# Four GNN layers on one core: rows without links on 49 dense groups by index, the rest of them in idle link slots

## The reference

```
edge_index = jnp.stack([src, dst])
x = _layernorm(x + _L0_gnn_ref(x, edge_index, ...))
x = _layernorm(x + _L1_gnn_ref(x, src, dst, ...))
x = _layernorm(x + _L2_gnn_ref(x, edge_index, ...))
x = _layernorm(x + _L3_gnn_ref(x, edge_index, ...))
```

## Time and profile before

| | |
|---|---|
| timed runs | 6511.86, 6522.25, 6542.76 us (median 6522.25) |
| span of the profiled execution, first to last instruction | 6136.9 us |
| median less the span | 385.4 us |
| TensorE, VectorE, ScalarE, GpSimd busy | 5167.8, 4560.9, 3817.9, 3041.7 us |
| mean granted TensorE clock | 0.886 |

### The profile page before, as it was taken

The page is one execution under the profiler, slowest core; times in us unless marked ns, Lnnn a source line. Parts: engine busy times, 40 slices in busy tenths (PEclk is TensorE's granted clock), DMA queues, the critical chain, the costliest instruction groups (busy, mean ns, idle before and its releaser), DMA issues. The chain is left out here.

```text
span 6136.9 us, 94789 instructions
## 1 busy us (share of the span) xinstructions
PE 5167.8 (84%) x23690; PEld 3888.2 (63%) x23690; DVE 4560.9 (74%) x13038; ACT 3817.9 (62%) x11901; POOL 3041.7 (50%) x2581
## 2 busy tenths in 40 slices
PE   2788899999999988888888998988899989945654
PEld 1566666666677776767666666667777767733443
DVE  7676655555677787887787888878878777768886
ACT  0587765666899766666655555565555567755555
POOL 1677777422444455555355665543333230057776
PEclk7899999999999999999988888889999989955555
DMA  1577543343566554545344444434544431134442
GB/s 49 183 266 255 193 136 113 125 142 112 195 221 220 184 183 165 190 171 183 137 141 155 157 154 159 161 109 141 166 153 152 137 109 54 39 115 138 139 138 94
DMA packets 362734, 925.74 MB, mean 151 GB/s; under 512 B 66872, under 2 KB 140715, under 8 KB 362198
## 3 DMA queue, kind: packets, MB, share of 16 engines
q1 hardware_dynamic: 271078, 702.73, 33.4%
q0 software_dynamic: 91120, 216.96, 12.1%
HBM read 568.39 MB, written 361.72 MB: 152 GB/s over the span
## 5 line engine op out<-in xcount | busy, mean ns | idle before, releaser
L2207 POOL DMA_INDIRECT got<-hop,end_i x600 | 642.6, 1071 | 725.0 <-PE psum L1014 466.0
L2207 POOL DMA_INDIRECT got<-tab,end_i x600 | 702.8, 1171 | 441.7 <-PE psum L1122 266.7
L1122 PE MATMUL psum<-got,sf 128*128 128x264 f32 (+2 forms) x1200 | 470.4, 482 | 365.0 <-DVE got L1946 288.4
L1014 PE MATMUL psum<-got,sf 128*128 128x256 f32 x1600 | 507.1, 399 | 104.8 <-ACT got L1278 96.8
L1122 PEld LDWEIGHTS psum<-got,sf 128*128 128x128 f32 x1200 | 238.8, 240 | 470.6 <-DVE got L1946 350.4
L1014 PEld LDWEIGHTS psum<-got,sf 128*128 128x128 f32 x1600 | 289.5, 195 | 269.4 <-issue 99.8
L2298 POOL DMA_INDIRECT out<-res,out_i x200 | 211.4, 1057 | 463.9 <-DMA out<-hd 358.0
L963 PE MATMUL psum<-h_t,w 128*128 128x512 f32 x784 | 380.3, 616 | 68.5 <-DVE h_t L1705 68.5
L1162 ACT ACTIVATE squares<-res,l_sv 128x256 f32<-128x256 f32 x600 | 297.3, 496 | 223.7 <-DVE l_sv L1851 188.7
L1278 ACT COPY got<-psum 1x256 f32<-1x256 f32 x796 | 280.0, 352 | 239.2 <-PE psum L1014 184.2
L1316 ACT ACTIVATE res<-res,l_mo 128x256 f32<-128x256 f32 x600 | 310.8, 589 | 147.7 <-DVE l_mo L1839 147.5
(11 more groups left out here) (438 smaller groups left out, 14914.2 us busy)
## 6 DMA issues: line engine op xcount, KB each, us to landing
own<-hop SPq DMA_DIRECT2D x150, 512.0 KB
x_t<-res SPq DMA_DIRECT2D x150, 512.0 KB
xo<-x_t SPq DMA_DIRECT2D x150, 512.0 KB, 3.7
hop<-res SPq DMA_DIRECT2D x100, 512.0 KB
x_in<-in_x SPq DMA_DIRECT2D x98, 512.0 KB, 4.6
out<-hd SPq DMA_DIRECT2D x98, 512.0 KB
tab<-tab SPq DMA_DIRECT2D x50, 536.0 KB, 2.7
own<-tab SPq DMA_DIRECT2D x50, 536.0 KB
```

The lines of the kernel that those rows point to most:

```text
L1014: T.matmul(o, sf_of(q)[:, k * P:(k + 1) * P], got_of(q)[:, k * FEAT:(k + 1) * FEAT], start=(p < 3), stop=True).then_inc(at("l_agg"), 1)
L1122: T.matmul(bank(3 + k % 2)[:, 0:g.ext], sf_[:, k * P:(k + 1) * P], got_of(q)[:, k * g.width:k * g.width + g.ext], start=True, stop=True).t ...
L2207: eng.indirect_dma_start(out=dst, out_offset=None, in_=table, in_offset=bass.IndirectOffsetOnAxis(ap=idx, axis=0), bounds_check=rows_ - 1, ...
```

## The change

1. `nd` falls from 98 to 49: `nd = ceil((n - 126 * 200) / 512)`. A list `ulist` of the rows without links is made at run time. Its first 25,088 rows are the dense groups; they are fetched and written by index, by GpSimd: `xin` and `dst` are each four indirect DMAs in place of one SyncE transfer.
2. The other rows without links (about 5,200) are put into link slots that are not the last of their destination. `rank_t` tells which; in pass 0 a compare (`oh`), four matmuls of one column (`oh`) and two additions (`node`) turn ranks into row numbers `node_i` and `out_i`, per link group, ahead of `own`.
3. So that a hosted row sees its loop alone: the 0/1 matrix gets a second half (`s8` and its DRAM copy are twice as wide; `sel` compares twice, `selm` reads the second half), and `hostc` is added to the loop logits (`es`, and one more operation in `sl`).
4. The picking of edges is three streams: `l` (links), `u` (rows without links, new), `o` (old loop table), each of ten `pack` steps on 586 words, with 10 indirect DMAs each. The weights are prepared behind them, in small parts. Dense groups wait for `wz`, for `uct` and for all `emito`.
5. The first `out` no longer waits for dense stores.

```diff
-    nd = -(-n // ROWS)
+    nd = -(-(n - (LINKS - 1) * nt) // ROWS)
-    ready = ("V", "prep", 0)
+    ready = ("V", "wz", 0)
-        if d >= 2:
-            add(("Y", "xin", d), 0.4, [("T", "x0", d - 2), ("T", "x1", d - 2)], landing=4.0)
+        add(("G", "xin", d), 4.8, [ ("T", "x0", d - 2), ("T", "x1", d - 2)], landing=2.5)
-            add(("T", "x", d), 0.6, [("Y", "xin", d), ready], ...)
+            add(("T", "x", d), 0.6, [("G", "xin", d), ("V", "uct", 0), ready] + [("G", "emito", i) for i in range(bits)], ...)
-        add(("Y", "dst", d), 0.35, [("S", "ln", d)] + ..., landing=3.0)
+        add(("G", "dst", d), 4.8, [("S", "ln", d)], landing=2.5)
...
+    stream("l", -1.0, [("Y", "edges", 0), ("G", "prep", 0)], -1.0)
+    stream("u", -0.9, [("V", "edgesl", 0)], -0.9)
+    stream("o", 0.3, [("V", "edgesu", 0)], -0.8)
...
+                put(("Y", "rnk", q), 0.4, s + prior("Yrnk") + ..., landing=4.0)
+                put(("V", "oh", q), 0.65, here("Yrnk") + ...)
+                put(("T", "oh", q), 1.2, here("Voh") + [("V", "uct", 0)], bank="ring", emptied=here("Vnode"))
+                put(("V", "node", q), 0.35, here("Toh"))
-                put(("G", "own", q), 5.2, s + prior("Gown") + gone(b, used), landing=2.5)
+                put(("G", "own", q), 5.2, s + here("Vnode") + prior("Gown") + gone(b, used), landing=2.5)
-                put(("V", "sel", q), 0.68, ...)
+                put(("V", "sel", q), 1.37, ...)
-                over = [("Y", "dst", d) for d in range(max(0, nd - 3), nd)] if i == 0 else [("G", "out", q - 1)]
+                over = [("G", "out", q - 1)] if i else []
...
+        def gpsimd_dense(eng, name, d):
+            if name == "xin":
+                if d >= 2:
+                    eng.wait_ge(at("t_fill"), fill_no["x1", d - 2] + 1)
+                eng.wait_ge(at("w_ready"), 2)
+                eng.wait_ge(at("d_clear"), 1)
+                for k in range(K):
+                    gather(eng, a["x"], x_in[:, d % 2, k, :], dn_i[:, d * K + k:d * K + k + 1], n, at(f"d_xin{d % 2}"))
+            else:
+                eng.wait_ge(at("d_ln"), d + 1)
+                for k in range(K):
+                    eng.indirect_dma_start(out=out, out_offset=...dn_i..., in_=hd[:, d % 3, k, :], ...)
...
             elif name == "selm":
-                if p == HOPS:
-                    for k in range(K):
-                        S.mul(to_sm[:, k, 1:P], sel[:, k, 1:P], lastc[:, k, i:i + 1])
-                else:
-                    S.copy(to_sm[:, :, 1:P], sel[:, :, 1:P])
-                S.copy(to_sm[:, :, 0], col0[:, :, i]).then_inc(at("l_sm"), 1)
+                S.copy(sm[:, par, :], s8_half(q, 1)).then_inc(at("l_sm"), 1)
...
             elif name == "out":
                 eng.wait_ge(at("l_ln"), ln_of(q) + 1)
-                if i == 0:
-
-                    for d in range(max(0, nd - 3), nd):
-                        eng.wait_ge(at(f"d_st{d % 3}"), 16 * (d // 3 + 1))
```

More of the change, by code:

```diff
@@ L219, in schedule @@
[L219 to L226, removed]
@@ L227, in schedule, with stream @@
-    add(("Y", "rows0", 0), 0.5, [("G", "emit", i) for i in range(bits)], landing=4.0, **first)
-    add(("V", "rowsa", 0), 5.3, [("Y", "rows0", 0)], **first)
+    def stream(s, rank, after, before):
+        add(("V", "edges" + s, 0), {"l": 8.5, "u": 6.5, "o": 4.5}[s], after, rank=before)
+        for k in range(bits):
+            add(("V", "pack" + s, k), 2.8, [("V", "pack" + s, k - 1) if k else ("V", "edges" + s, 0)], rank=rank)
+        base_ = [("V", "basu", 0)] if s == "u" else []
+        add(("V", "place" + s, 0), 4.0 if s == "l" else 3.2, [("V", "pack" + s, bits - 1)] + base_, rank=rank)
+        for i in range(bits):
+            if i:
+                add(("V", "cut" + s, i), 0.5 + (1.3 if s == "l" else 0.7) * 2 ** (bits - 1 - i) / 512,
+                    [("V", "cut" + s, i - 1) if i > 1 else ("V", "place" + s, 0)], rank=rank)
+            add(("G", "emit" + s, i), 1.3, [("V", "cut" + s, i) if i else ("V", "place" + s, 0)] + ([("Y", "prep", 0)] if s != "o" else []), rank=rank, landing=2.5)
@@ L234, in schedule @@
     add(("T", "rows2", 0), 3.0, [("V", "rows1", 0)], rank=-1.0)
[L235 to L238, removed]
+    add(("V", "rows2", 0), 3.4, [("V", "rows1", 0)], rank=-1.0)
+    add(("V", "rows3", 0), 1.2, [("V", "rows2", 0)], rank=-1.0)
@@ new lines, in schedule @@
+    add(("G", "rows3", 0), 9.0, [("V", "rows3", 0), ("Y", "rows1", 0), ("V", "edgesu", 0), ("V", "edgeso", 0)], rank=-1.0)
+    add(("Y", "uload", 0), 0.4, [("G", "emitu", i) for i in range(bits)], rank=-0.9, landing=3.0)
+    add(("V", "dn", 0), 0.4, [("Y", "uload", 0)], rank=-0.9)
+    add(("G", "uc", 0), 4.8, [("G", "emitu", i) for i in range(bits)] + [("V", "rks", 0)], rank=-0.9, landing=2.5)
+    add(("T", "uct", 0), 0.6, [("G", "uc", 0)], rank=-0.9, bank="ring", emptied=[("V", "uct", 0)])
@@ L240, in schedule @@
+    took = {0: 0.7, 1: 0.45, 2: 0.9, 3: 3.0, 4: 0.4, 5: 0.7, 6: 0.45, 7: 0.7, 8: 0.45}
+    for f, (length, after) in fills.items():
+        add(("T", f"wf{f}", 0), length, after, bank="ring", emptied=[("V", f"we{f}", 0)], **late)
+        add(("V", f"we{f}", 0), took[f], [("T", f"wf{f}", 0)], **late)
+    add(("V", "wb", 0), 3.6, [("V", "we2", 0)], **late)
+    add(("V", "wz", 0), 14.0, [("V", "dn", 0)] + [("V", f"we{f}", 0) for f in fills], **late)
     chunk = {p: ("T", "hop3") if p < HOPS else ("T", "agg3") for p in range(7)}
-    dense_parts(plan, nd)
+    dense_parts(plan, nd, bits)
@@ L287, in schedule @@
                 b = ring("s8", q)
-                put(("V", "sel", q), 0.68, here("Yrec") + gone(b, {0: [("Y", "s8st"), ("S", "sel")]}))
+                put(("V", "sel", q), 1.37, here("Yrec") + gone(b, {0: [("Y", "s8st"), ("S", "sel")]}))
                 put(("Y", "s8st", q), 0.35, here("Vsel"), landing=3.0)
@@ L294, in schedule @@
                 b = ring("s8", q)
-                put(("Y", "s8", q), 0.4, s + prior("Ys8") + gone(b, {x: [("S", "sel")] for x in range(7)}), landing=4.0)
+                put(("Y", "s8", q), 0.4, s + prior("Ys8") + gone(b, {x: [("S", "sel")] + [("S", "selm")] * (x >= HOPS) for x in range(7)}), landing=4.0)
                 ready = here("Ys8")
@@ L2192, in gpsimd_rows @@
[L2192 to L2204 removed]
+            if s == "u" and i == 0:
+                eng.wait_ge(at("r_pad"), 48)
```

923 lines of the change are left out of this document (545 added, 378 removed).

## The result

| | kernel before | changed kernel | ratio, 95% interval |
|---|---|---|---|
| first comparison (chip not recorded), median | 6538.6 us (5 runs) | 6179.7 us (5 runs) | 0.9458 [0.9416, 0.95] |
| one more comparison, on chip 3 | 6154.0 us (9 runs) | 5729.7 us (5 runs) | 0.9322 [0.9308, 0.9336] |
| profiled execution, span | 6136.9 us | 6221.5 us (first), 5721.8 us (chip 3) | |

A forecast was written before the change was run, and what follows sets the result against it. TensorE was taken as the bound from pass 1 on, GpSimd in pass 0. Stage terms summed to 5630 us, 507 below the profiled span; 6522 - 507 gave 6015 us, range 5870 to 6160, or 5790 to 6210 with A, D and start bounds.

The forecast's parts named there:

- The constant: Around the profiled span: the median of the runs is 385.4 us above 6136.9 us, and that difference was kept.
- Start, 225: Before pass 0: third stream and reordered packing make VectorE's serial work about 185 us; 225 us, +20, bounds 180 and 290.
- Pass 0, 600: Pass 0: GpSimd is full and sets its length, no dense group gets a turn, additions cost 0; stays at 600 us.
- Pass 1, 590: Pass 1: leftover `end`s outrank dense work, 3 groups instead of 12; 574 us, taken as 590 for TensorE's low clock.
- my own price: Dense group beside link work: at most 20.4 us of TensorE, from the drain, divided by TensorE's busy share in pass 1.
- Pass 2, 424: Pass 2: GpSimd alone gives 285 us without dense groups; 13 groups at 10.7 us each add 139.
- Drain and pass 6: End: 436 us drain gone; pass 6 takes 787 for 50 groups, 30 for three dense groups, 10 and 32: 859 us.
- Rival A: Pass 0: dense groups do get turns; 20 there add 212 us, save 400 elsewhere, about 5830 us; chance 0.13.
- Rival B: Passes 1 to 5: TensorE's clock falls with thin dense work; gain gone at mean clock about 0.81; chance 0.05.
- Rival C: GpSimd in series: all 98 dense transfers on the path bring back 521 us, 6536 us, no change; chance 0.04.
- Rival D: Dense groups starve to the end, half in a drain behind pass 6 at 22.9 us each: 6165 us; chance 0.10.
- The rule on the port: Busy VectorE can keep GpSimd from writing descriptors: 392 indirects take some 86 us more of GpSimd; not used in the sum.

The follow-up runs named there:

- Without `end`: Changed kernel without its 200 `end` gathers, slots made from the source's row number, chip 3: 5680.2 us, ratio 0.9237.
- without `own`: Changed kernel without `end` gathers and with pass 0's indirect `own` loads replaced by four SyncE loads a group, chip 3: 5526.7 us, ratio 0.8985.
- bare pass: Pass of the kernel before with 5 of its 98 dense groups, the old link stream alone, chip 2: 5686.3 us, ratio 0.8638.
- the kernel with half of the groups: Kernel before with 49 of its 98 dense groups, loads and stores still by SyncE, no hosted rows, chip 1: 5975.6 us, ratio 0.9149.
- the first spread kernel: Changed kernel with dense loads paced in the planner, 6, 6, 9, 10, 9 and 9 groups in passes 1 to 6, chip 2: 6399.3 us, ratio 0.9701.
- the new kernel: Changed kernel with 5 of its 49 dense groups, the new link stream alone, chip 1: 5793.0 us, ratio 0.8859.

## Why the prediction was right or wrong

The time was inside the range, and 2.7% off, but that it came so near is luck: the stages of the sum are 548 us short of the median span of the first comparison (6177.6 for 5630), and the 385 us of a frame that does not exist covered most of it. Chip 3 shows the sum without the frame:

| | forecast | chip 3 | first profile |
|---|---|---|---|
| start | 225 | 160 | 159 |
| passes 0, 1, 2 | 600, 590, 424 | 630, 696, 470 | 713, 892, 598 |
| passes 3, 4, 5 | 1035, 1059, 838 | 1062, 1069, 851 | 1076, 1094, 886 |
| pass 6 and end | 859 | 784 | 803 |
| span | 5630 | 5722 | 6221 |
| beside it | 385 | 2 | 2 |

- **The constant.** "The median of the runs is 385.4 us more ... I keep that difference" is the step that failed. It was the difference between a quick and a slower chip, and it lies in passes 0 and 1 (337 of 409 us). The changed kernel pays on such a chip 83, 196 and 128 us in passes 0 to 2, 407 in all, and so the wrong constant stood in for a real cost. As a saving I forecast 507 us; the chips show 359 (first comparison) and 424 (chip 3).
- **Start, 225.** The price of a `pack` step was right (2.67 us for 2.7), the sum not: VectorE's serial work is 133 us before the first `hop`, not 185, because the third stream and the weights run on into pass 0, where VectorE is busy 34%. Off by -65.
- **Pass 0, 600.** Right: no dense group, GpSimd waits for "issue", TensorE near half clock. 630: `own` now waits 13.4 us for `res`, and the `o` stream's ten stores stand behind the first of them (176.8 to 189.8 us). Without `end` it is 586, without `own` 470. That the 19.5 dense groups cost nothing there fits chip 3 (600 with them, 630 without); on the slower chips they did cost: 822 us with 19.5, 693 with one, 7.0 each.
- **Pass 1, 590.** The largest miss within a chip, +106. The step that failed is "I take 3 groups near its end". The dense loads did wait for the last `end`, as I had it, but that one starts at 1147.7 us, half way through the pass, and 7.5 groups came. With 7.5 my own price, 20.4 / (730 / 767) = 21.4 us, gives 767 - 4.5 x 21.4 = 671, and 687 with the 16 us for the clock: 9 from the measured 696. The price itself, taken from the drain, is 71 us for 4.5 groups here, 15.8 each, if nothing else of the change counts in this pass. On chips 1 and 2 it is far off: 12 groups are worth 882 - 802 = 80 us in pass 1, 6.7 each, and with 4.5 groups fewer the changed kernel is no quicker there (892). The prediction had named the price as the term it would fail by.
- **Pass 2, 424.** The floor of 285 was GpSimd's alone; a bare pass takes 376 us on chips 1 and 2, with TensorE at clock 0.50. So the 17 groups cost about (467 - 376) / 17 = 5.4 us each, not 10.7, and not evenly: it is the last ones that are free. With transfers by SyncE the pass takes 376 us without a group, 475 with 13.5 (the kernel with half of the groups) and 481 with 17; on chip 3 it takes 470 with 12 and with 17. Therefore neither 13 nor 12 groups would have brought the 43 us that I forecast. By index on the slower chips none is free: 378, 483 and 598 us with 0, 6 and 17 groups. 17 groups instead of 13 came, since GpSimd still had time for them.
- **Passes 3 to 5.** Right on chip 3 within 50 us together. GpSimd's 10.6 us a group are cheap there, not free: +27 in pass 3 with nearly as many groups as before (13 for 13.5), and on the slower chips 17 of 32 us went when SyncE took the transfers. Pass 5 was right by two errors: 3 groups came, not 8, and it is not shorter for that, since groups cost nothing there (851 us with 3, 852 with 9).
- **Drain and pass 6.** Right, and nearly the whole gain: the wait is gone, no group is left over, and 50 link groups take 15.0 us each instead of 15.7, with no 30 us for three dense groups. -75.
- **TensorE** is busy 4420 us, not 4150: the change took off 748 us, 15.3 for each of 49 groups.

Rival A is refuted as a gain: with dense groups in pass 0 the kernel is slower. Rival B did not come: the mean clock of passes 1 to 5 is 0.93 on chip 3 and 0.90 in the first profile (the lengths and clocks of the tables), above its 0.81. But the clock is part of why dense groups were worth less than their TensorE time: without them a `hop` matmul of pass 2 takes 707 ns, with 17 of them 395. The Trainium skill, "TensorE: Matmul & The Clock Gate", section "HAM oscillation — how this bites in real kernels", says that gaps between bursts of matmuls put the array back to its low rate; the bare pass 2 agrees, at 0.50 and with TensorE idle 133 of 376 us between link matmuls, and pass 1, where I had looked for it, does not show it (0.98 with 7.5 groups). Rival C did not come on chip 3, as far as pass 2 shows it; on the others the dense indices cost 2.7%, a third of its 521 us. Rival D did not come by itself; the first spread kernel made it, and a group in the last stage costs 28 us there, more than D's 17.7 to 22.9. The rule on the port: the 196 `x_in` loads take 208.7 us, 1.06 us each (tile view of chip 3, 210.5 us less a clearing of 1.8), so its 86 us would be nearer 15; it did not matter.

## What to carry to other kernels

Hold a profile against timed runs of the same chip before adding what is "around" it; a gap of 6% between span and time is a sign that they are not the same execution, not a constant. Take the price of a work group from the place it will leave, and don't take it for the same along the way: the end gave 388 us when the groups behind the link work went, while a group beside link work was worth nothing (pass 5, and the last five of pass 2) to 16 us (pass 1 on chip 3). A stage whose busiest engine works 96% of the time need not shrink with that engine's work: pass 2 took 467 us with 17 dense groups and still 376 us with none, where its link matmuls ran at half the clock. Work moved to GpSimd's queue costs by what stands behind it and not by its busy share: 1.39 us of time for each added indirect where the engine was idle a third of the time and more (chip 2; 0.31 for each taken away on chip 3).

## What the runs showed of the hardware

- One program, three chips: 6154, 6546 and 6595 us for the kernel before. The profiles of the two slower ones show TensorE completions that come from 1 to over 20 us after the records, most of all in pass 0 (48 to 71% of 200), and lack 11 to 17% of the 1400 records of such completions. But a bare pass 2, 200 gathers in 376 us, shows them in 6% (378 us and 15% in the new kernel), so the density of GpSimd's transfers alone is not the rule.
- The Trainium skill, "NOTIFIC — the notification-queue block", section "Overflow: three behaviours, one of which stalls the engine", says that the recording path inside the block holds engines back rather than lose a record, and that neither of its overflow bits was ever seen set in the authors' measurements. If such a stall is what makes completions late, the slower chips' times are partly the recording's; no run here shows it, since every run has its recorded span.
- 200 indirect DMAs in passes 0 and 1 cost 1.39 us each where added on chip 2 and 0.31 each where taken away on chip 3 ((44 + 18) / 200). Whether the chip or the direction makes the difference is not shown.
- The clock of link matmuls alone: 400 `hop` matmuls take 707 ns each in a bare pass 2 (granted clock 0.50) and 395 ns in the same pass with 17 dense groups (0.98).
